# One block for norm, keys, values and queries, and another interleaving in the first attention

## The reference

```
x = x + L0_xattn(layernorm(x), ctx, ctx, ...)     # changed
x = x + L0_ffn(layernorm(x), ...)                 # the rest is the same
x = x + L1_xattn(ctx, layernorm(x), mask, ...)
x = x + L1_ffn(x, ...)
```

```
r_k = rk_table[clip(key - query, -128, 128) + 128]     # [1024, 77, 16]; r_v likewise
attn = softmax((qh.kh + qh.r_k) / sqrt(16))
out = (attn.vh + sum_k attn * r_v) @ Wo.T + bo
```

## Time and profile before

| | us |
|---|---|
| median of 3 runs | 2106.36 |
| profiled execution | 2103.89 |
| its span | 2102.1 |
| PE busy | 1899.3 (90%) |
| DVE busy | 1325.7 (63%) |
| ACT busy | 1023.1 (49%) |
| POOL busy | 619.8 (29%) |
| first instruction of the projections' block on PE | 19.93 |
| first instruction of the attention's block on PE | 42.99 |
| first instruction of the router's block | 266.33 |

### The profile page before, as it was taken

The page is one execution under the profiler, slowest core; times in us unless marked ns, Lnnn a source line. Parts: engine busy times, 40 slices in busy tenths (PEclk is TensorE's granted clock), DMA queues, the critical chain, the costliest instruction groups (busy, mean ns, idle before and its releaser), DMA issues. The chain is left out here.

```text
span 2102.1 us, 40117 instructions
## 1 busy us (share of the span) xinstructions
PE 1899.3 (90%) x13658; PEld 1645.5 (78%) x13659; DVE 1325.7 (63%) x2970; ACT 1023.1 (49%) x1757; POOL 619.8 (29%) x555
## 2 busy tenths in 40 slices
PE   6888948999569999999999999999999985999994
PEld 3567948999468887888888888888888864999994
DVE  5373065676668877887787778877877875222223
ACT  3543315555246555554555555555555642444441
POOL 3200012333145432442244324432443201122220
PEclk9999959999679999999999999999999995999997
DMA  6502072111333113311322133113311209111114
GB/s 207 178 37 108 33 271 91 45 50 45 115 71 72 41 32 73 72 41 33 71 65 48 32 72 71 41 33 71 72 38 35 64 18 351 54 38 37 35 35 133
DMA packets 93711, 159.24 MB, mean 76 GB/s; under 512 B 22433, under 2 KB 54879, under 8 KB 91755
## 3 DMA queue, kind: packets, MB, share of 16 engines
q1 hardware_dynamic: 82923, 134.32, 22.7%
q0 software_dynamic: 8320, 20.65, 3.2%
q10 hardware_dynamic: 2304, 2.10, 0.3%
HBM read 71.57 MB, written 32.41 MB: 49 GB/s over the span
## 5 line engine op out<-in xcount | busy, mean ns | idle before, releaser
L1864 ACT ACTIVATE a_prob<-a_slot,a_npeak 128x848 f32<-128x848 f32 x256 | 248.5, 971 | 205.2 <-DVE a_npeak L1925 204.7
L1730 PE MATMUL a_slot<-a_KHL,a_QHL 128*128 128x424 f32 (+1 forms) x1536 | 299.0, 343 | 13.0 <-DVE a_probT L1946 11.2
L1923 DVE TENSOR_REDUCE a_part_peak<-a_slot 128x2 f32<-128x848 f32 x256 | 265.5, 1037 | 39.7 <-PE a_slot L1730 39.7
L1877 ACT ACTIVATE a_probT<-a_slot 128x640 f32<-128x640 f32 x256 | 180.6, 705 | 198.7 <-PE a_slot L1739 152.4
L1755 PE MATMUL a_po<-a_probT,a_V 128*64 128x256 f32 (+1 forms) x2304 | 276.8, 385 | 0.0
L1730 PEld LDWEIGHTS a_slot<-a_KHL,a_QHL 128*128 128x128 f32 x1536 | 236.9, 190 | 39.2 <-issue 13.3
L1739 PE MATMUL a_slot<-ident,a_prob 128*128 128x128 f32 x2048 | 266.9, 274 | 0.0
L1955 DVE CUSTOM_DVE_ANT_0 a_masked<-a_prob,a_maskr,a_latent_sum 128x253 f32<-128x253 f32 x256 | 182.8, 714 | 102.6 <-ACT a_prob L1866 86.9
L1739 PEld LDWEIGHTS a_slot<-ident,a_prob 128*128 128x128 f32 x2048 | 234.4, 142 | 8.7 <-issue 0.3
L1755 PEld LDWEIGHTS a_po<-a_probT,a_V 128*64 128x64 f32 (+1 forms) x2304 | 153.8, 136 | 83.3 <-issue 7.2
L1680 PEld LDWEIGHTS a_side<-a_W,a_latT 128*128 128x128 f32 x1536 | 195.0, 197 | 24.3 <-issue 10.8
(11 more groups left out here) (321 smaller groups left out, 3028.1 us busy)
## 6 DMA issues: line engine op xcount, KB each, us to landing
a_KHL<-a_KT SPq DMA_DIRECT2D x128, 256.0 KB, 4.5
a_QHL<-a_QT SPq DMA_DIRECT2D x128, 128.0 KB, 2.4
m_up<-_L_ffn_gate_up_proj_dram SPq DMA_DIRECT2D x8, 1024.0 KB, 9.0
m_up<-in_L_ffn_W_dram SPq DMA_DIRECT2D x8, 1024.0 KB, 9.2
m_down<-in_L_ffn_W_dram SPq DMA_DIRECT2D x8, 1024.0 KB, 12.6
a_prob_dram<-a0p_zeros SPq DMA_DIRECT2D x4, 1632.0 KB, 10.6
a_dist_dram<-a_dist SPq DMA_DIRECT2D x4, 1632.0 KB, 8.1
a_band_prob<-a_prob_dram SPq DMA_DIRECT2D x4, 1632.0 KB, 7.2
```

Of the source, the lines that this page charges most:

```text
L1730: ins = t_.matmul(out[:, i * BANK:i * BANK + hi - lo], q, KHL[:, pair.parity, h, part, lo:hi], start=part == 0, stop=part == 1)
L1864: a_.activation(prob[:, u % 2, 0:2 * CUT].rearrange("p (n k) -> p n k", n=2), two_banks(slot[u % 2]), ACT.Exp, bias=bias, accum_out=latent ...
L1877: a_.activation(probT[:, u // 4 % 2, HALF:KT_TILES, h, u % 2 * P:(u % 2 + 1) * P], slot[u % 2][:, HALF * P:KT_TILES * P].rearrange("p (t q ...
L1923: v.tensor_reduce(part[:, 0:2], two_banks(slot[u % 2]), AX.X, ALU.max).then_inc(part_peaked, 1)
```

## The change

Blocks 1 and 2 become one. `residual_norm` becomes a class `ResidualNorm` whose parts (statistics, normalise, turn, copy) are called from the engines' programs between the projections. The turned buffers in PSUM go from 4 to 2 and the query banks from 4 to 3. PE makes keys, values, turns the first four tiles, and then the queries by groups of tokens, with the turns of the next group after each group's first half.

The loads are ordered by use, and each consumer waits for its own: x group 0, Wk, context, x group 1, Wv, identity, bk, bq, Wq, x groups 2 and 3, then bv, rv0, mask, relk, the context prelude's nine, Wo, bo.

`rv` is cleared by POOL, not by DVE. `zeros` is [128, 204], and each store to `prob_d` reads it 16 times. SP doesn't wait for the stores' landing at the block's end; the attention's SP does, ahead of the first store of probabilities. Of the 25 small DMAs that pack the far values, 15 are issued by SP in this block and 10 by POOL in the attention's. Only one of the four parts of `kblock` is made here, the other three by DVE beside value tiles 0 to 2.

In the attention the band's scores are cut in eight halves of a tile. The first stands at the start, the others beside value tiles. `SCORED` in the diff names what PE makes at (value tile, round): b is a half of the band, s a score; `SOFT` names in the same way what ACT does. Scores after a near tile wait for the four adds that read `ps` (`s_read`), not for the whole shift. The near tiles stand at places 7, 10, 13 and 15 of `value_order`, and at 7, 10, 13 and 14 of `soft_order`. The exp of a near tile is two instructions. POOL adds the output's bias to all of `xres` once, and `add_outputs` is one addition instead of two.

```diff
             @block.sync
             def _(sp):
+                norm.load(sp, 0)
+                weight("Wk", W["Wk"], k_loaded)
+                sp.dma_start(ctxT[:, :, :], ...).then_inc(k_loaded, 16)
+                norm.load(sp, 1)
+                weight("Wv", W["Wv"], v_loaded)
+                sp.dma_start(ident[:, :], I["ident"]).then_inc(ident_loaded, 16)
...
                 sp.wait_ge(tails, 1)
-                sp.dma_start(rv[:, :, :, GROUP - 1, 0:D0], I["rel_v"]).then_inc(rv_loaded, 16)
+                sp.dma_start(rv[:, :, :, GROUP - 1, 0:D0], I["rel_v"]).then_inc(rest_loaded, 16)
+                sp.wait_ge(v_cleared, 1)
+                sp.wait_ge(v_made, BATCH)
+                place_values(sp, PLACES[:PLACED_FIRST], v_set)
                 sp.wait_ge(zeroed, 1)
                 for n in range(NN):
-                    sp.dma_start(prob_d[n].rearrange("p j h -> p (j h)"), zeros[:, :]).then_inc(cleared, 16)
-                sp.wait_ge(cleared, 16 * NN)
-                sp.wait_ge(rv_loaded, 16)
+                    sp.dma_start(prob_d[n].rearrange("p j h -> p (j h)").rearrange("p (h j) -> p h j", h=H0),
+                                 zeros[:, :].unsqueeze(1).to_broadcast([P, H0, BAND])).then_inc(cleared, 16)
+                sp.wait_ge(rest_loaded, 48)
...
-        value_order = far_tiles + near_tiles
+        value_order = far_tiles[:7] + near_tiles[:1] + far_tiles[7:9] + near_tiles[1:2] + far_tiles[9:11] + near_tiles[2:3] + far_tiles[11:12] + near_tiles[3:4]
+        soft_order = far_tiles[:7] + near_tiles[:1] + far_tiles[7:9] + near_tiles[1:2] + far_tiles[9:11] + near_tiles[2:4] + far_tiles[11:]
+        SCORED = {(0, 1): "b1", (0, 2): "s2", (1, 1): "b2", (1, 2): "s3", (2, 1): "b3", (2, 2): "s4", (3, 1): "b4", (3, 2): "s5", (4, 0): "s6", (4,
+                  2): "s7", (5, 1): "b5", (5, 2): "s8", (6, 2): "b6 s9", (7, 1): "b7", (7, 2): "s10", (7, 11): "s11", (8, 2): "s12", (9, 2): "s13",
+                  (10, 4): "s14", (12, 2): "s15"}
...
+            def bands(k):
+                n, half = divmod(k, 2)
+                t = near_tiles[n]
+                banks_read(scored)
+                for j in range(SB):
+                    if k:
+                        pe.wait_ge(d_out, SB * (k - 1) + j + 1)
+                    g, h = divmod((half * SB + j) * DHEADS, GROUP)
+                    nc.tensor.matmul(ps[:, j, 0:DHEADS * BAND], QT[:, g, t * P:(t + 1) * P],
+                                     rblock[:, n % NEAR, h:h + DHEADS, :],
+                                     start=True, stop=True).then_inc(d_done, 1)
...
+            shear_scores(0)
+            shear_scores(1)
+            shear_probabilities(0)
+            shear_scores(2)
+            shear_scores(3)
+            for n in range(1, NN):
+                shear_probabilities(n)
```

More of the change, by code:

```diff
@@ L83, in after @@
         self.engine.wait_ge(self.sem, self.n)
[L86 to L161, removed]
@@ L482, in _, with shear_scores @@
         def _(sp):
-            for n in range(NN):
+            def shear_scores(n):
                 sp.wait_ge(d_out, DGROUPS * (n + 1))
@@ L597, in project_outputs @@
                 ins.then_inc(y_done, 1)
+            scored = banded = 0
+            bands(0)
+            banded = 1
             scores(0)
-            scores(ahead[0][0])
+            scored = 1
+            scores(1)
+            scored = 2
             pe.wait_ge(padded, 1)
-            pe.wait_ge(v_placed, 16 * len(PLACES))
             turn(0)
+            pe.wait_ge(v_placed, 16 * len(PLACES[PLACED_FIRST:]))
+            pe.wait_ge(v_set, 16 * PLACED_FIRST)
             for n, (i, r, blocks) in enumerate(ROUNDS):
@@ L611, in _ @@
                     turn_outputs(i - 1)
-                if r == 1 and len(ahead[i]) == 2:
-                    scores(ahead[i][1])
                 if r == 2 and i:
                     project_outputs(i - 1)
-                if n + 1 == round_ends[value_order[i]] and i + 1 < TILES and ahead[i + 1]:
-                    scores(ahead[i + 1][0])
+                for what in SCORED.get((i, r), "").split():
+                    k = int(what[1:])
+                    if what[0] == "b":
+                        bands(k)
+                        banded = k + 1
+                    else:
+                        scores(k)
+                        scored = k + 1
             turn_outputs(TILES - 1)
@@ L622, in _, with copy_bands @@
         def _(act):
-            for k in range(NN * DGROUPS):
-                act.wait_ge(d_done, k + 1)
-                n = k // DGROUPS
-                if k % DGROUPS == 0 and n >= 2:
+            def copy_bands(k):
+                n, half = divmod(k, 2)
+                if half == 0 and n >= 2:
                     act.wait_ge(d_stored[n % 2], 16 * (n // 2))
-                h = k % DGROUPS * DHEADS
-                nc.scalar.activation(dist[:, n % 2, :, h:h + DHEADS].rearrange("p j h -> p h j"),
-                                     ps[:, k % SB, 0:DHEADS * BAND].rearrange("p (h j) -> p h j", h=DHEADS),
-                                     ACT.Copy).then_inc(d_out, 1)
@@ L633, in soft @@
-            def soft(i):
-                t = soft_order[i]
-                act.wait_ge(s_shift, i + 1)
-                if t not in near_tiles and far_tiles.index(t) >= 3:
-                    act.wait_ge(t_done, round_ends[far_tiles[far_tiles.index(t) - 3]])
-                dst = (near_prob[:, near_tiles.index(t)].rearrange("p k h -> p h k") if t in near_tiles else
-                       prob[:, prob_slot[t], 0:H0 * CTX].rearrange("p (h k) -> p h k", h=H0))
-                nc.scalar.activation(dst, shifted[:, :, :], ACT.Exp).then_inc(p_done, 1)
+                for j in range(SB):
+                    act.wait_ge(d_done, SB * k + j + 1)
+                    h = (half * SB + j) * DHEADS
+                    nc.scalar.activation(dist[:, n % 2, :, h:h + DHEADS].rearrange("p j h -> p h j"),
+                                         ps[:, j, 0:DHEADS * BAND].rearrange("p (h j) -> p h j", h=DHEADS),
+                                         ACT.Copy).then_inc(d_out, 1)
@@ L655, in _ @@
                                              ACT.Copy).then_inc(ot_out, 1)
[L656 to L659 removed]
+                for what in SOFT.get((i, r), "").split():
+                    k = int(what[1:])
+                    if what[0] == "b":
+                        copy_bands(k)
+                    else:
+                        soft(k, (0,) if what[0] == "e" else (1,))
             act.wait_ge(ot_done, TILES)
```

294 lines of the change are left out of this document (196 added, 98 removed).

## The result

The changed kernel takes 2092.03 us (median of 4 runs, 2088.43 to 2101.08), the one before 2108.08 (4 runs beside them): ratio 0.993, 95% interval 0.9907 to 0.9952. The forecast was 2093, range 2083 to 2103. The execution that was profiled is the slowest of the four: 2101.08, with a span of 2099.3, only 2.8 under the 2102.1 of before. So I read the stages in both and lean on no single one.

The account below looks back on a forecast made before the run. PE bounded the near tiles; alternating scores and shifts through one `ps` held the far ones. Start +2, attention -14.8, one addition -0.4: -13.2 from 2103.9, 2090.7, median 2093.2; range 2083 to 2103.

Parts of the forecast that it names:

- `vones` ready at 22: Merged block: after the norm and its later loads, `vones` is ready at 22 us, with 2.4 us added (bounds 0 and 5).
- Queries, copies and context done by 36 to 37: Merged block: PE's queries end near 33.5 us; the last copies and the context's transposes make it 36 to 37.
- The small DMAs, 6.5 us: Merged block, behind `vones`: SP issues 15 small DMAs at 0.43 each, 6.5 us (bounds 5 and 13).
- The zeros hold SP for 16 us: End of merged block: SP gets 1000 to 2000 runs ahead, then issues as the queue drains at 338 GB/s; 16 us.
- The start, T = 45: The attention's start: 22 + 6.5 + 16 = 44.5, plus 0.5 for the barrier, 45 against 43.0: plus 2.
- held much longer: Rival, chance 0.11: small DMAs take 12 us and zeros 24, so the attention starts at 58.5; 2106.7.
- The attention, minus 14.8: From the attention's start to the last weigh's end: T + 203.5, where it was T + 218.3.
- the band's wait: First near tile, value tile 7: its band arrives at T + 87.5, PE stands from 84.8, 2.7 us (bounds 0 and 8).
- tile 15: Last value tile in the attention, a near one: given 19.7 us, the last weigh ending at T + 203.5.
- SP is not held: Rival, chance 0.22: the queue takes 8192 runs without a stall, the block ends at 37, 8 earlier; 2085.2.
- The clock falls: Rival, chance 0.05: clock 0.70 in value tiles 0 to 6 makes 65 us into 93; plus 21, 2114.
- POOL's packing: Attention's head: POOL issues its 10 packing DMAs by T + 9, first needed at T + 16, so not late.

Follow-up runs that it names:

- z_late: The changed kernel with SP issuing the four zero stores at the start of the attention's block, not at the end of the merged one; 2079.3 us, ratio 0.9875.
- again: The changed kernel, unchanged, run once more for a second trace; 2090.18 us, ratio 0.9929; its profiled execution took 2081.65.
- after: The changed kernel itself, in its first runs and profile; 2092.03 us, ratio 0.993 against the kernel before.
- merge_only: The changed kernel's merged block, but the attention in the old order (band first and whole, far tiles, then near); 2115.49 us, ratio 1.0037.
- place0: The changed kernel with all 25 small packing DMAs issued by POOL in the attention, none by SP; 2091.17 us, ratio 0.9923.
- z_runs3264: The changed kernel with each zero store reading a zeroed 3264-byte row 4 times, 512 runs a store, the same bytes; 2089.22 us (one run).
- z_runs13056: The changed kernel with each zero store reading a full zeroed row of 13056 bytes, 128 runs a store, the same bytes; 2085.68 us, ratio 0.9907.
- z_later18: As z_late, but SP issues the zeros only once POOL's packing has landed and places 18 small DMAs, not 15; 2075.15 us, ratio 0.9843.

## Why the prediction was right, and where only its sum was

The sign came out, and by the steps named: SP's issue holds the start, and the new order wins more than that costs. The time came out by luck, because two errors of size cancel: the start is some 9 us later than I said, the attention at full clock some 10 shorter. Either error alone would have put the time at about 2102 or 2084, the edges of the range.

**`vones` ready at 22.** It was 22.76. DVE's statistics and normalising run on from 5.5 to 20.9. The last eight normalising instructions take 4.30 us, against 2.83 before: one of them takes 1.85, beside POOL's clearings of `rv` and `vpacked` from 17.83 to 19.76.

**Queries, copies and context done by 36 to 37.** 38.1. It didn't matter here; in z_late it is what sets T, 39.16.

**The small DMAs, 6.5 us.** Mis-sized: 12.73, 0.85 each. I had the number in hand, as POOL's 0.8 for the same transfers, named it as the upper bound of 13, and took a value near that of the plain loads instead. Here an issue's price went with the transfer, not with the engine that makes it. Plus 6.2 on the sum.

**The zeros hold SP for 16 us.** The step was right, and it was the one that was in doubt: 18.60, 16.83, 17.57 and 17.35 in four kernels that issue them there, 3.30 to 4.18 with fewer runs. By the Trainium skill's page DMA: Bandwidth & Descriptors, section Anatomy of one DMA, the generation of descriptors is small and a lot can be emitted before its cost shows; this is written of POOL's path, not of SP's. The two kernels with up to 2048 runs in all agree with it, at 0.8 to 1.05 us an issue; those with 8192 do not. But the 16 was reached by two wrong numbers. The drain was 207 GB/s, not 338, and SP got further ahead than I said. In the 18.6 us 18.6 x 207 = 3.85 MB of 6.68 moved, so 2.83 MB, some 3500 runs of 816 bytes, were still queued when SP came free (an estimate; I said 1000 to 2000). The same working at the end of the second issue, 2.81 us after the first began, gives some 3400, and at the end of the third some 3600. That fits a queue that is full from the second store on. At 338 GB/s and 3500 runs it would have been 11 us; at 207 and 1500, 26.

**The start, T = 45.** 54.93 and 53.28: 8 to 10 late, of which 6.2 are the small DMAs, 0.7 the later `vones`, the rest the zeros. This is the failed term. T is nearer to the 58.5 of the rival "held much longer" than to my 45.

**The attention, minus 14.8.** By its pieces, in the profiled execution: half band 1 at T + 18.7 (18), the cycle 9.84 (10.0), score 5 done at T + 55.3 (55), the band's wait 2.57 (2.7) until T + 88.9 (87.5), last weigh T + 203.9 (203.5). This looks like agreement throughout and is not. In `again`, at clock 1.00 behind the first 20 us, the wait ends at T + 83.7 and the last weigh at T + 193.9. At full clock my sum was 10 us too long. About 4.3 of it is tile 15: I gave it 19.7, as a near tile with its successor's work in it, but the last tile has none, and the rows show 15.4 (232.60 to 247.96, from one turning of outputs to the next; before, 246.75 to 262.16, 15.4 as well, a row of the trace that I did not use):

```profile
246.75 0.38 PE L589 MATMUL a_py<-ident,a_O 128*128 128x128 f32 x2
...
262.16 0.44 PE L589 MATMUL a_py<-ident,a_O 128*128 128x128 f32 x2 [0.86 <-DVE a_O L693]
```

```profile
232.60 0.38 PE L647 MATMUL a_py<-ident,a_O 128*128 128x128 f32 x2
...
247.96 0.44 PE L647 MATMUL a_py<-ident,a_O 128*128 128x128 f32 x2 [0.81 <-DVE a_O L777]
```

1.4 more is tile 12, 6.8 instead of 8.2 between the same marks: the wait for `normalise` that I carried over as 1.4 is 0.8 and falls ahead of that stretch. The rest, 3.8, lies ahead of T + 87.5, where I let half band 1 and its successors come later than they do, and the band's wait last longer. What the profiled execution has on top goes with its lower clock: 4.3 us by the band's wait, 9.2 by the router, counted from the first weigh in both.

Of the signs that I named, T near 45 failed. The issues behind the first were not 4 to 5 us each but 2.2, 7.2 and 8.5. The half bands 10 us apart and the one wait of 2 to 3 us for the band came out (2.57; 1.60 in `again`), and so did PE's 95% from 147 us on, at clock 0.97 in one execution and 1.00 in the other.

**Sum.** Predicted 2 - 14.8 - 0.4 = -13.2. Measured, with T from the two profiles and the attention at full clock, 11 - 24 - 0.4 = -13.4; with the clock's patches as in the first profile, 12 - 14.4 - 0.4 = -2.8, the profiled span. The medians say -16. So the median run seems to be one in which the clock mostly holds; this is an inference, since only two executions were traced (over the whole run the granted clock is 0.942 in those of 2101.08 and 2094.13 us, 0.946 in those of 2088.43 and 2089.92). The forecast was met because I put the start 9 us too early and made the attention 10 us too long. Nor is all of a span the change's: in `again` it is 22.2 us shorter than before, of which 14.7 lie ahead of the router and 7.5 behind it, where nothing was changed.

**The rivals.** "SP is not held" is refuted for this change by all four profiles with 8192 runs ahead of the barrier (`after`, `again`, merge_only, place0); z_late shows what it would have brought, and more: 2079, where I had 2085. "Held much longer" was right on the small DMAs, at 0.85 each, not on the zeros. "The clock falls" is not the bound, but it is there: from 0 to 10 us an execution, in patches behind waits of 1.8 to 2.6 us; I had priced it as all or nothing. What decides in one execution that the clock falls behind a wait and in the next that it stays up, the runs don't show; this stays open. The forecast's own range had 4 us for stalls and nothing for the clock, which takes up to 10.

**What I didn't list** was POOL's packing. I had its ten DMAs issued by T + 9 and "not late". Beside the draining zeros they land after 7.7 us (median), against 2.0 for the quickest in place0 when the engines were free, and PE stands for them at the first weigh 1.27 us in the changed kernel, 0.28 in `again`, 2.9 in z_runs3264, 3.50 in z_late, 6.00 in z_runs13056 and 7.6 in place0.

## What to carry to other kernels

To drop the wait for a DMA's landing at the end of a block is worth nothing while the block must still wait for an issue that lasts as long (here 18.60 us in place of 13.9): move the issue itself past the barrier, and behind whatever small transfers are needed first. Price a strided store by its runs as well as its bytes: a repeated source that saves 2.4 us of POOL's clearing, and the 2.7 us for which that clearing held VectorE and the small DMAs behind it, cost 15 us of SP here. And where a forecast has two halves, run each alone: one of these cost 0.4%, the other made the whole gain. The half that cost could then be mended: with the stores moved, the merged block brings 0.9875 and 0.9843, against 0.9928 for the order alone.

## What the runs showed of the hardware

- SP issues a first store of 2048 runs of 816 bytes in 0.61 us, the second in 2.2, the third in 7.2 and the fourth in 8.5, at a drain of 207 GB/s: by the estimate above it gets about 3500 such runs ahead. With 512 or 128 runs a store the four took 4.18 and 3.30 us.
- The same 6.7 MB left at 207 to 221 GB/s in runs of 816 bytes and at 326 GB/s (with the small transfers beside them) in runs of 13 KB; DMA's share was 1.01 to 1.04 and 0.91.
- SP pays 0.85 us for the issue of one of the small strided packing transfers, as POOL does (0.80).
- TensorE's granted clock is lower behind some waits and not behind the same waits in another execution of the same program: 4.00 and 2.31 us for the same score behind the same 1.79 us, at 0.76 and 1.00. Other kernels of the same order show both: 3.87 in z_late, 2.31 in z_runs3264, z_runs13056, place0 and z_later18. After 18 us of standing the first half band took 4.95 us (clock 0.67 over its first 6 us), after 1.49 us 2.98 (1.00).
- Some VectorE instructions stand while POOL clears: one on 128x2 took 1.63 us before, ending with POOL's clearing of the wide `zeros`, and 0.16 in the changed kernel, where POOL does nothing at that moment; a normalising one took 4.62 us in z_runs3264, 1.85 in the changed kernel and 0.41 otherwise.
